# A four-layer graph network on one core: the last layer placed in one block with the scatter before it, and its input made by groups of nodes

## What is computed

```python
x = _layernorm(x + L0(x, adj))             # adj @ (x W) + b
x = _layernorm(x + L1(x, adj))             # mean over neighbours, W, relu
x = _layernorm(x + L2(x, adj))             # two pruned-hypergraph iterations, H = adj
...
# end of one L2 iteration
agg = H_pruned.T * dv_isqrt[None, :] @ transformed
agg = agg * de_inv[:, None]
msg = dv_isqrt[:, None] * (H_pruned @ agg)
x = relu(msg @ Theta)
...
# L3, the last layer
support = input @ weight
mask = (adj != 0)
rank = cumsum(mask, axis=1)
deg = rank[:, -1:]
k = minimum(deg, 100)
pos = rank - (deg - k)
w = mask * where(pos > 0, 0.5 ** (k - pos), 0.0)
out = w @ support + bias
x = _layernorm(x + out)
```

## Time and profile before

| what | value |
|---|---|
| median of 3 runs | 2440.88 us (2438.64 to 2444.03) |
| the profiled execution, its time | 2440.41 us |
| its span | 2438.5 us |
| instructions | 36215 |
| bytes moved | 834.18 MB, 342 GB/s in the mean |
| mean granted TensorE clock | 0.932 |

### The profile page before, as it was taken

One profiled execution on the slowest core, in us unless ns is written; L12 is line 12 of the kernel. 1 busy time (PEld: TensorE's weight loads), 2 busy tenths in 40 slices (PEclk: granted clock), 3 DMA queues, 4 the chain that ended last, 5 costly groups with the idle time before them and its releaser, 6 DMA issues. The chain is left out here.

```text
span 2438.5 us, 36215 instructions
## 1 busy us (share of the span) xinstructions
PE 2055.7 (84%) x15608; PEld 732.7 (30%) x15608; DVE 1757.7 (72%) x2037; ACT 779.8 (32%) x990; POOL 4.5 (0%) x18
## 2 busy tenths in 40 slices
PE   6798959989977766699999989987676689996897
PEld 2224324323221111143344323221111134334333
DVE  7875982268879999965541348879999975553998
ACT  0001000146644333311111036653333311111897
POOL 0000000000000000000000000000000000000000
PEclk9999989999988888899999999988888899997999
DMA  9975989989939999987779989929999987763796
GB/s 385 421 336 233 427 356 425 427 328 376 373 132 424 420 411 410 370 317 277 276 278 386 427 326 376 379 106 411 412 411 410 375 330 270 269 252 156 311 421 253
DMA packets 123486, 834.18 MB, mean 342 GB/s; under 512 B 8512, under 2 KB 10560, under 8 KB 76608
## 3 DMA queue, kind: packets, MB, share of 16 engines
q1 hardware_dynamic: 121136, 829.48, 85.0%
q10 hardware_dynamic: 2192, 2.40, 0.3%
HBM read 695.54 MB, written 136.31 MB: 341 GB/s over the span
## 5 line engine op out<-in xcount | busy, mean ns | idle before, releaser
L923 ACT ACTIVATE stream<-stream,negmax 128x4096 f32<-128x4096 f32 x128 | 475.2, 3713 | 521.4 <-DVE negmax L917 521.4
L912 DVE CUSTOM_DVE_ANT_0 stream<-ps,stream 128x1024 f32<-128x1024 f32 x352 | 413.9, 1220 | 55.3 <-PE ps L876 31.9
L876 PE MATMUL ps<-edgeT,node_twice 64*128 64x512 f32 x1024 | 281.0, 669 | 183.5 <-DVE mx L912 183.4
L455 PE MATMUL ps<-stream,stage 128*64 128x512 f32 x1728 | 387.8, 600 | 42.8 <-DMA stream<-in_adjT 27.4
L876 PE MATMUL ps<-edgeT,query_twice 64*128 64x512 f32 x1024 | 249.6, 619 | 6.3 <-DVE edgeT L944 4.0
L1209 PE MATMUL ps<-stream,xw 32*64 32x512 f32 x4096 | 230.5, 595 | 3.7 <-issue 3.0
L455 PEld LDWEIGHTS ps<-stream,stage 128*64 128x64 f32 x1728 | 122.1, 138 | 300.6 <-issue 221.5
L876 PEld LDWEIGHTS ps<-edgeT,node_twice 64*128 64x128 f32 x1024 | 94.2, 201 | 377.9 <-DVE mx L912 267.6
L894 PE MATMUL ps<-stream,ones 128*1 128x512 f32 x1024 | 185.4, 862 | 11.1 <-DVE stream L1249 11.1
L1249 DVE SCALAR_TENSOR_TENSOR stream<-stream,cut 128x4096 f32<-128x4096 f32 x40 | 179.4, 4484 | 1.4
L1427 DVE SCALAR_TENSOR_TENSOR query_twice<-stream,query_twice 128x512 bf16<-128x512 f32 x256 | 154.7, 679 | 4.6 <-ACT query_twice L1405 4.5
(11 more groups left out here) (195 smaller groups left out, 1692.9 us busy)
## 6 DMA issues: line engine op xcount, KB each, us to landing
stream<-in_adj SPq DMA_DIRECT2D x136, 2048.0 KB, 13.0
stream<-in_adjT SPq DMA_DIRECT2D x74, 2048.0 KB, 13.2
pruned<-stream SPq DMA_DIRECT2D x64, 2048.0 KB, 10.5
spare<-in_adj SPq DMA_DIRECT2D x26, 2048.0 KB, 10.3
spare<-pruned SPq DMA_DIRECT2D x22, 2048.0 KB, 11.5
query_twice<-pruned SPq DMA_DIRECT2D x22, 2048.0 KB, 11.3
node_twice<-pruned SPq DMA_DIRECT2D x20, 2048.0 KB, 11.5
query_twice<-in_adj SPq DMA_DIRECT2D x14, 2048.0 KB, 15.7
```

Of the source, the lines that this page charges most:

```text
L455: last = nc.tensor.matmul(ps[F * h:F * h + F, bank + b, :], stage[:, t.k % SL, :], half_bank(src, b, h), start=False, stop=False, skip_gro ...
L876: last = nc.tensor.matmul(ps[:, 2 * slot + h, :], stationary[F * h:F * h + F, rows_n], bank_of(edgeT[F * h:F * h + F, :], c), start=True, ...
L912: nc.vector.tensor_tensor_reduce(out=prod[s][:, cols], in0=ps[:, 2 * slot:2 * slot + 2, :].rearrange("p a b -> p (a b)"), in1=block_in[:, ...
L923: nc.scalar.activation(prod[s], prod[s], ACT.Exp, bias=negmax[:, s:s + 1], accum_out=zsum[:, s:s + 1]).then_inc(exp_done, 1)
```

## The change

The phase "l3" goes. Its program (`last_layer`) becomes further parts of the block that holds the scatter, with no barrier between. The groups are taken in the order `TURN` = (3, 2, 0, 1): units go from the last row block downwards, so units 0 to 15 use groups 3 and 2 of `support` alone (and units 32 to 47 again). The message matmuls come in that order, and each group's message, residual sum and centring follow at once. The pair (3, 2) is normalised before group 0 is centred, is folded, projected and split after unit 0's weighting. The pair (0, 1) is centred before unit 0, its variance follows unit 1, its scaling unit 2, its folds stand before units 3 and 4, its projections before units 6 and 7, its splits after units 9 and 10; unit 16 waits for them. There are six places for blocks, `slot` 2, 3, 7, 0, 1, 4, and three blocks are sent after `scattered` = 7, three after `scattered` = 8. At the end of the first iteration, VectorE's wait for its own messages is dropped.

```diff
+        TURN = (3, 2, 0, 1)
...
+            def centre_part(self, do, y, k):
+                v = nc.vector
+                do(v.reduce_sum(part(st["mean"], k), part(y, k), AX.X))
+                do(v.tensor_scalar(part(st["mean"], k), part(st["mean"], k), 1.0 / F, None, ALU.mult))
+                v.tensor_tensor(part(y, k), part(y, k), per_node_part(st["mean"], k), ALU.subtract)\
+                    .then_inc(self.centred, 1)
...
-            return stream[:, s, :].rearrange("p (n c) -> p n c", n=2)
+            return slot[(2, 3, 7, 0, 1, 4)[s]].rearrange("p (n c) -> p n c", n=2)
...
+        def last_layer(block, sem, next_ahead, norm, msg_taken):
...
+            SL, QC = 6, 4
...
+                norm.square_part(act, res, 0)
+                norm.square_part(act, res, 1)
+                norm.pair_root(act, 0)
+                clean_unit(0)
+                take_fold(0)
+                take_fold(1)
+                take_support(0)
+                norm.square_part(act, res, 2)
+                take_support(1)
+                norm.square_part(act, res, 3)
+                for u in range(1, units):
+                    clean_unit(u)
+                    if u == 2:
+                        norm.pair_root(act, 1)
+                    if u in (4, 5):
+                        take_fold(u - 2)
+                    if u in (7, 8):
+                        take_support(u - 5)
...
+                    if u == 0:
+                        split_support(0)
+                        split_support(1)
+                    if u == 1:
+                        norm.pair_variance(dve, do, 1)
+                    if u == 2:
+                        norm.pair_scale(dve, do, res, 1)
+                    if u in (9, 10):
+                        split_support(u - 7)
...
+                pe.wait_ge(starts_loaded, 16)
+                pe.wait_ge(msg_taken, 4)
+                begin(0)
+                fold_part(0)
+                fold_part(1)
+                support_part(0)
+                support_part(1)
+                for u in range(units):
+                    if u == NB:
+                        begin(1)
+                    if u in (3, 4):
+                        fold_part(u - 1)
+                    if u in (6, 7):
+                        support_part(u - 4)
+                    for q in range(2):
+                        for h in range(2):
+                            halve(u, 2 * q + h)
+                        if q == 0 and u in (0, 16, 24):
+                            pe.wait_ge(sup_split, {0: 2, 16: 4, 24: 4}[u])
+                        last = add(u, q)
+                    last.then_inc(summed, 1)
...
-                        for done, slots_free in ((groups - 1, (2, 3)), (groups, (0, 1))):
-                            sp.wait_ge(scattered, done)
-                            for s in slots_free:
-                                sp.dma_start(two_half_blocks(s), half_blocks(s)).then_inc(next_ahead[s], 16)
+                        sp.wait_ge(scattered, groups - 1)
+                        for m in range(3):
+                            if m == 2:
+                                sp.wait_ge(turned, groups * CH - 2)
+                            sp.dma_start(two_half_blocks(m), half_blocks(m)).then_inc(next_ahead[m], 16)
+                        sp.wait_ge(scattered, groups)
+                        for m in range(3, 6):
+                            sp.dma_start(two_half_blocks(m), half_blocks(m)).then_inc(next_ahead[m], 16)
...
-                    if last_it:
-                        do(v.tensor_tensor(res[:, :, :], res[:, :, :], cur[:, :, :], ALU.add))
-                        norm.centre(do, res)
-                        norm.variances(dve, do)
+                    for i, k in enumerate(TURN):
+                        do(message(i, k))
+                        do(v.tensor_tensor(part(res, k), part(res, k), part(cur, k), ALU.add))
+                        if i == 2:
+                            norm.pair_scale(dve, do, res, 0)
+                        norm.centre_part(do, res, k)
+                        if i == 1:
+                            norm.pair_variance(dve, do, 0)
+
+                if last_it:
+                    last_layer(block, sem, next_ahead, norm, msg_taken)
```

More of the change, by code:

```diff
@@ L176, in loads_ahead @@
         def loads_ahead(name):
-            return [nc.alloc_semaphore(f"{name}_row_block_loaded{s}") for s in range(5 if name == "l3" else 8)]
+            return [nc.alloc_semaphore(f"{name}_row_block_loaded{s}") for s in range(8)]
         nat4 = ps[:, 0:4, :].rearrange("p b (k f) -> p (b k) f", f=F)
@@ L284, in __init__ @@
                 self.var_ready, self.std_ready = sem("var_ready"), sem("std_ready")
+                self.scaled = sem("scaled")
             def scalar(self, act, centred):
@@ L1072, in build @@
                 msg_taken, out_ready, out_taken = sem("msg_taken"), sem("out_ready"), sem("out_taken")
-                next_ahead = loads_ahead("l3" if last_it else f"i{it + 1}_edge")
+                next_ahead = [sem(f"last_layer_loaded{s}") for s in range(7)] if last_it else loads_ahead(f"i{it + 1}_edge")
                 norm = LayerNorm(sem) if last_it else None
@@ L1230, in _ @@
                     pe.wait_ge(msg_taken, 4)
-                    for pair in ((0, 8), (24, 16)):
+                    for pair in ((24, 16), (0, 8)) if last_it else ((0, 8), (24, 16)):
                         for k in range(8):
@@ L1234, in _ @@
                                 h, m = divmod(place(n + k), 16)
-                                last = nc.tensor.matmul(nat4b[:, n + k, :], accT[F * h:F * h + F, P * m:P * m + P],
+                                at = 8 * TURN.index(n // 8) + k if last_it else n + k
+                                last = nc.tensor.matmul(nat4b[:, at, :], accT[F * h:F * h + F, P * m:P * m + P],
                                                         theta[F * h:F * h + F, :], start=True, stop=True)
@@ L1297, in _ @@
                         nc.scalar.copy(by_place[:, q], ps[:, q, :].rearrange("p (m r) -> p m r", r=32))                            .then_inc(msg_taken, 1)
-                    if last_it:
-                        for k in range(4):
-                            act.wait_ge(norm.centred, k + 1)
-                            nc.scalar.activation(part(tmp, k), part(res, k), ACT.Square).then_inc(norm.squared, 1)
                 @block.gpsimd
```

262 lines of the change are left out of this document (141 added, 121 removed).

## The result

| | before | changed |
|---|---|---|
| median | 2439.95 us (4 runs, 2438.64 to 2444.03) | 2429.65 us (4 runs, 2428.06 to 2431.95) |
| ratio | | 0.9958, 95% interval 0.9940 to 0.9975 |
| profiled execution, its time and span | 2440.41, 2438.5 | 2431.95, 2430.2 |
| first message operation to unit 0 | 20.39 | 15.01 |
| first message operation to unit 2 | 44.12 | 26.43 |

The changed kernel is 10.3 us faster in the medians (6 to 15 us by the interval) and 8.3 us in the span of its profiled execution. The forecast was 2431.4 us, a gain of 9.0. The stretch, which is the part that was changed, is 9.3 us shorter; that profile lost 0.8 of it again because its first message operation came at 2225.17 instead of 2224.35, behind code that computes the same in both.

The account below looks back on a forecast made before the run. VectorE, with ScalarE also full, bounds the loop at 2.41 us a unit, so only the way in can shorten: 16.9 - 5.25 - 2.65 = 9.0 us gained, 2440.4 to 2431.4 us, range 2428.3 to 2436.0.

Parts of the forecast that it names:

- Points 1 to 3: First message operation to unit 0: four groups, first pair's variance and scaling, phase end replaced by a change of part; 15.5 us.
- Points 4 and 5: Unit 0 at 2.45 us, then splits of two groups at 3.6 us, with their casts ready beforehand.
- Point 6: Unit 1 stalls as today, 4.1 us, then second pair's sums of squares, 1.55; unit 2 at 27.2 us, 16.9 gained.
- Point 7: VectorE's work moved into the loop: reciprocal and two scalings 1.65, two splits 3.6; no room, so 5.25 us lost.
- Point 8: Side work of ScalarE (1.85 us) and TensorE (0.8 us) in the loop's units 3 to 8; together 2.65 us lost.
- The edits at nothing: New block places and earlier loads, and the wait dropped at the end of the first iteration: put at no effect.
- The busy TensorE row: TensorE busy 39.76 of 40.00 us in the loop; read as no spare time, stalls are 5.45 us and the gain 6.2.
- stalls in full: Rival: side work in the loop stalls in full, 5.95 us; gain 5 to 6, 2434.4 to 2435.5 us; chance 0.13.
- hidden: Rival: TensorE's and ScalarE's side work in the loop is hidden; gain 11.7, 2428.8 us; chance 0.08.
- Nothing waited for a load: Rival: loads become the loop's bound, each block falling back 0.16 us; up to 4.2 comes off, 2435.6 us; chance 0.03.
- The clock, the rival for a slower kernel: Gaps in the first units keep TensorE at 1.2 GHz; eight such units make it 4.9 us slower; chance 0.03.
- its ring: The loop's cycle weigh, halve, clean, weigh across the engines; its slack was to forgive about 0.5 us once.

## Why the prediction was right, point by point

The sum held: 9.0 forecast, 9.3 in the stretch, 10.3 in the medians. Two errors cancel in part: the way to unit 2 gained 0.8 us more than forecast, the loop lost 0.5 more.

- Points 1 to 3, to unit 0: 15.5 forecast, 15.01 measured. A message that doesn't depend on the operation before it starts 0.61 us after it, the reciprocal of a pair takes 0.25 instead of 0.35, and the change of part, put at 0.3, shows no idle time ahead of unit 0.
- Points 4 and 5, unit 0 and two splits: 6.05 forecast, 5.98 measured (2240.18 to 2246.16). The splits found their casts ready.
- Point 6, unit 1: 4.1 forecast and measured (2246.16 to 2248.97 + 1.29), then 1.34 for the variance instead of 1.55. The way to unit 2 became 26.43 instead of 27.2, a gain of 17.7 where 16.9 was forecast.
- Point 7, VectorE's side work: 5.25 forecast, 5.1 measured. It is paid in full. The 5.4 us by which the loop without the others' side work is longer than before hold 0.33 of wait in unit 2 besides.
- Point 8, the stalls: 2.65 forecast, 2.95 measured by leaving their causes out. The size was right by luck of its parts: taken out alone, ScalarE's part was worth 0.36 us, not 1.85, and TensorE's 1.60, not 0.8; the other 1.0 us either of them is enough for. The step that failed is the claim that ScalarE, having no room, pays each operation in full, while most of TensorE's is absorbed. A projection group took 1.16 us in the loop (1.0 to 1.37 assumed), and after each of the two VectorE waited (0.54 and 0.90). While it waits, ScalarE finds time for its own copies and casts: with TensorE's part gone they cost 1.35 us, with it there 0.36.
- The edits at nothing: right for the places (186.59 against 186.62). The wait dropped at the end of the first iteration lies ahead of the stretch, and no run tests it.
- The busy TensorE row: taken as it stands it gave 5.45 us of stalls. Measured were 2.95. TensorE's operations from unit 4 on (0.66, 1.16 and 1.16 us, 2.98 in all) cost 1.6 to 2.6 us, so TensorE did have some room under a busy share of 99%, though less than the forecast gave it. By the rule of the Trainium skill (Trainium Kernel Development and Optimization, Performance Expectations), that matmul busy time misleads because matmuls are pipelined, the sum stayed at 9.0; the runs agree with it.

Of the rivals, "stalls in full" would have taken 5.95 us; "hidden" needs none; both are out. Nothing waited for a load. The clock, the rival for a slower kernel, cost little more than before:

```profile
2246.10:2249.00 2.90, 2.70 (x14) 1.25 (x16) 1.37 (x4) 0.74 (x2) 0.00 (x0) 0.50 0.00 0
2249.00:2251.50 2.50, 2.50 (x16) 1.04 (x14) 2.47 (x5) 1.63 (x3) 0.00 (x0) 0.50 0.29 39
2251.50:2254.00 2.50, 2.50 (x22) 1.22 (x20) 2.16 (x5) 1.65 (x5) 0.00 (x0) 0.84 0.79 295
2254.00:2284.00 30.00, 26.01 (x210) 11.77 (x206) 27.32 (x46) 24.54 (x42) 0.00 (x0) 1.00 0.84 323
```

TensorE is at half clock while it adds unit 0 and the first half of unit 1, much as before, and at full clock from 2254 on, through all the side work. The clock rose within unit 2 instead of at its start; that is the wait of 0.34 us, and no further unit ran at half clock. (In that rival's sum eight units at half clock come to 8 x 1.8 - 9.0 = 5.4 us slower, not 4.9.) What point 6 put down to the additions of unit 0 alone, the 1.5 us stall of unit 1, is in the main the half clock at which they are made: when TensorE added unit 0 at full clock, VectorE waited 0.58 us in all.

What the prediction did not see is that the change defers work that is better done first. Its own rows had it: VectorE had no idle time in the loop to hide anything, but 2.5 us of it around unit 1. And the second pair's folds and projections, done first, keep TensorE busy until it adds unit 0, which then goes at the full clock.

## What to carry to other kernels

When an engine is the bound of a loop, work of its own that is moved into the loop is paid in full. Work of the others in its ring costs less where the bound engine pauses: here 1.5 instead of 2.95 us. Put the deferred steps into the holes that are there (here VectorE's wait around unit 1), but look first at why a hole is there: this one was mostly TensorE at half clock after a pause, and two steps of VectorE in a row ahead of a unit made TensorE pause again. Cut the serial way into a loop into parts, so that the bound engine always has another part to go on with. Judge such an edit by the stretch in the trace when whole runs scatter by more than the edit is worth, and check an in-order engine's list for a step that waits ahead of one that is urgent.

## What was not expected of the hardware

The same eight projections took 2.84 us in one execution (TensorE from 2236.99) and 3.78 in another, in the same place of the program. The windows over their last part, in the changed kernel and in the version with a split on each side of unit 1 (columns as in the earlier trace rows):

```profile
2238.40:2239.80 1.40, 1.40 (x12) 1.24 (x10) 1.30 (x4) 0.83 (x2) 0.00 (x0) 0.91 0.13 53
```

```profile
2239.00:2240.90 1.90, 1.87 (x9) 1.57 (x8) 1.83 (x4) 1.11 (x2) 0.00 (x0) 0.51 0.08 34
```

In the one the granted clock had gone back to full (0.91 in the mean), in the other it was still at half (0.51), with the same work before it. The changed kernel itself shows both: 2.84 us in its first profiled execution, 3.51 in its second. In the version with a split on each side of unit 1 the slow case was enough to turn a cast into a 1.02 us wait on VectorE. How fast TensorE was in the first units went with its pauses just before. In the changed kernel 4.37 us of pause stand ahead of the additions at half clock. In the kernels with both pairs ahead, pauses of 2.26, 3.13 and 1.81 us were followed by half clock (0.52, 0.50, 0.50) and by waits of VectorE; in the two with a split on each side of unit 1, whose pauses there were at most 1.43 us, the clock stayed at 1.00.

And the scatter of whole runs, up to 9 us in one comparison, probably lies ahead of the change: in the profiled executions the first message operation moves by 10 us, while the stretch repeats within half a microsecond.
